# A four-layer graph network: memory and queue order at the start of the attention scores

## The reference, cut to what matters

```python
h = jnp.maximum(_layernorm(x), 0.0)
for head in range(8):
    Wx = h @ Ws[head] + Wb[head]
    s = Wx[v_tgt] @ a_w[head, :64] + Wx[v_src] @ a_w[head, 64:] + a_b[head]
    s = leaky_relu(s, 0.2)
    alpha = segment_softmax(s, v_tgt)
    outs.append(segment_sum(alpha[:, None] * Wx[v_src], v_tgt))
x = x + concat(outs)
```

## Time and profile before

| | us |
|---|---|
| median of 3 runs without the profiler | 2629.58 (2628.07 to 2631.13) |
| span of the profiled execution | 3086.3 |
| scoring and softmax in the profiled execution | about 2121 to 2482 |
| busy in it: PE, DVE, ACT, POOL | 2384.8, 1593.7, 335.0, 1795.9 |
| mean granted TensorE clock | 0.896 |

### The profile page before, as it was taken

One profiled execution on the slowest core, in us unless ns is written; L12 is line 12 of the kernel. 1 busy time (PEld: TensorE's weight loads), 2 busy tenths in 40 slices (PEclk: granted clock), 3 DMA queues, 4 the chain that ended last, 5 costly groups with the idle time before them and its releaser, 6 DMA issues.

```text
span 3086.3 us, 32808 instructions
## 1 busy us (share of the span) xinstructions
PE 2384.8 (77%) x8542; PEld 1265.4 (41%) x8542; DVE 1593.7 (52%) x3774; ACT 335.0 (11%) x523; POOL 1795.9 (58%) x1878
## 2 busy tenths in 40 slices
PE   7888889887678777785788888885068589988887
PEld 5534444343223222221354454453058445544444
DVE  7665555554234353332244444444059677766665
ACT  4200000000000000000000000001057310000000
POOL 0466666665466666665666666653710456666665
PEclk9898999998789888997899999997579789999999
DMA  6586666676567766666666666663134457776665
GB/s 157 174 243 180 174 180 177 187 241 177 154 192 212 203 201 205 196 193 181 184 200 198 204 200 199 204 181 80 10 101 153 136 157 211 208 222 192 194 190 171
DMA packets 212761, 557.12 MB, mean 181 GB/s; under 512 B 55433, under 2 KB 56834, under 8 KB 212601
## 3 DMA queue, kind: packets, MB, share of 16 engines
q0 software_dynamic: 144448, 462.60, 52.3%
q1 hardware_dynamic: 66970, 90.10, 9.7%
q10 hardware_dynamic: 1182, 2.33, 0.3%
HBM read 515.28 MB, written 39.59 MB: 180 GB/s over the span
## 4 chain that ended last, share of the span: by engine, by line
PE 51%; DVE 15%; another core or an unknown queue 13%; issue 12%; DMA 6%; POOL 2%; ACT 1%; SPq 0%; ACTq 0%; DVEq 0%; POOLq 0%
PE tiles L1456 28%; DMA ring<-table,src_t 5%; PE upper L1416 5%; PE last_bank L1597 2%; PE tiles L1453 2%; PE tiles L1452 2%; DVE sel L776 2%; PE upper L1458 2%; PE last_bank L1416 2%; PE upper L1687 1%; POOL ring L1758 1%; PE upper L1626 1%; PE upper L1405 1%; DVE stage L713 1%
## 5 line engine op out<-in xcount | busy, mean ns | idle before, releaser
L1758 POOL DMA_INDIRECT ring<-table,src_t x1320 | 1266.9, 960 | 717.8 <-issue 324.3
L1456 PE MATMUL tiles<-ring,sel 128*125 128x512 f32 x2590 | 1390.4, 652 | 264.2 <-issue 178.4
L1456 PEld LDWEIGHTS tiles<-ring,sel 128*125 128x125 f32 x2590 | 444.3, 198 | 754.6 <-issue 745.5
L1813 POOL DMA_INDIRECT ring<-table,src_t x415 | 399.0, 961 | 240.5 <-PE upper L1458 105.5
L483 DVE TENSOR_TENSOR sel<-iota_bank,dl_t 128x500 f32<-128x500 f32 (+1 forms) x330 | 221.5, 674 | 513.3 <-PE tiles L1456 226.6
L1218 DVE TENSOR_TENSOR ring<-ring,last_bank 128x512 f32<-128x512 f32 x388 | 260.5, 685 | 169.6 <-DMA ring<-table,src_t 140.6
L1458 PEld LDWEIGHTS upper<-big,sel 128*125 128x125 f32 x880 | 169.7, 193 | 222.5 <-issue 222.0
L1452 PE MATMUL tiles<-ring,sel 128*125 128x512 f16 x440 | 176.5, 401 | 61.8 <-issue 32.1
L1453 PE MATMUL tiles<-ring,sel 128*125 128x512 f16 x440 | 172.9, 393 | 10.6 <-issue 10.3
L1416 PE MATMUL upper<-wh,hTh 128*125 128x512 f32 x200 | 100.4, 502 | 73.1 <-DVE hTl L759 23.7
L1791 POOL DMA_INDIRECT big<-score_table,src_t x104 | 98.4, 946 | 81.5 <-DVE acc L988 50.1
(11 more groups left out here) (335 smaller groups left out, 2522.2 us busy)
## 6 DMA issues: line engine op xcount, KB each, us to landing
ring<-table,src_t POOLq DMA_INDIRECT x1735
table<-stage SPq DMA_DIRECT2D x50, 224.0 KB
table<-acc SPq DMA_DIRECT2D x50, 224.0 KB
acc<-dst_places SPq DMA_DIRECT2D x28, 256.0 KB
x<-dst_places SPq DMA_DIRECT2D x27, 256.0 KB
x<-in_x SPq DMA_DIRECT2D x25, 224.0 KB
kept_x<-x SPq DMA_DIRECT2D x25, 224.0 KB
x<-kept_x SPq DMA_DIRECT2D x25, 224.0 KB
```

The lines of the kernel that those rows point to most:

```text
L1456: last = P.matmul(to, sel[:, n % SELS, :], rows, start=False, stop=True, skip_group_check=True)
L1758: G.indirect_dma_start(out=(ring16 if layer == 2 else ring)[:, n % RING, :], out_offset=None, in_=table[layer][:, :], in_offset=bass.Indir ...
L1813: G.indirect_dma_start(out=rows_at(i), out_offset=None, in_=table[3][:, :], in_offset=bass.IndirectOffsetOnAxis(ap=src_t[:, i:i + 1], axis ...
```

## The change

- A tensor `spare` (12288 bytes in each partition) is added, and all six one-hot buffers lie in it. Its room comes from the descriptors' scratch, which is now 4096 bytes.
- DVE: the wait for the store of tile 22 ahead of `src_hot(0)` goes, and that for tile 23 ahead of the loop. The four masks move from ahead of `u3` to behind `rows_out` of tile 24.
- ACT: the waits for the stores of tiles 20 and 21 go; those for 22 to 24 move to the first `edge_scores`. The waits for `cont_ok` and `g1_z` move behind `dst_hot(2)`.
- POOL: the wait for `pj_out` moves from ahead of all gathers to ahead of the 65th. (The gathers of groups 3 to 31 write memory that holds no weights of the last projection; those from W3_GROUP = 35 do.)
- SP: the wait for `x_kept` and loads 2 and 3 move ahead of the stores of tiles 21 to 24; load 4 stays behind them.

```diff
+    W3_GROUP = next(k for k in GATHERED if (k + 1) * UG * H > KB * D)
...
+        spare = sb("spare", [128, 6, D])
...
-        dp, sp, dp_hot, sp_hot = ([flat_acc[:, 2 * WR + (2 * n + q) * GW // 2:2 * WR + (2 * n + q + 1) * GW // 2].bitcast(BF16)
-                                   for q in range(2)] for n in range(4))
+        dp, sp = ([flat_acc[:, 2 * WR + (2 * n + q) * GW // 2:2 * WR + (2 * n + q + 1) * GW // 2].bitcast(BF16)
+                   for q in range(2)] for n in range(2))
...
-        dp_hot.append(flat_acc[:, 3 * WR:3 * WR + GW // 2].bitcast(BF16))
-        sp_hot.append(stage[:, 9 * TH:9 * TH + GW // 2].bitcast(BF16))
+        dp_hot, sp_hot = ([spare[:, 3 * n + q, :].bitcast(BF16) for q in range(3)] for n in range(2))
...
-            stored(V, 22)
+            for k in range(TILES - LATE, TILES - 2):
+                rows_out(k)
             src_hot(0)
-            for to, flag, end in ((cont, keep, 0), (cont_back, nlast, CE - 1)):
...
             V.wait_ge(u_in, 48)
...
             rows_out(TILES - 2)
             rows_out(TILES - 1)
-            stored(V, TILES - 2)
+            for to, flag, end in ((cont, keep, 0), (cont_back, nlast, CE - 1)):
...
-            stored(A, 20)
             dst_hot(0)
-            stored(A, 21)
             dst_hot(1)
-            A.wait_ge(cont_ok, 2)
-            A.wait_ge(g1_z, TILES)
-            for t in range(TILES - 3, TILES):
-                stored(A, t)
 
             def edge_scores(b, half):
                 h0 = half * 4
+                if b == half == 0:
+                    for t in range(TILES - 3, TILES):
+                        stored(A, t)
...
                     dst_hot(k + 2)
+                if k == 0:
+                    A.wait_ge(cont_ok, 2)
+                    A.wait_ge(g1_z, TILES)
...
-            G.wait_ge(pj_out, 3 * TILES)
             for k in GATHERED:
+                if k == W3_GROUP:
+                    G.wait_ge(pj_out, 3 * TILES)
...
+            S.wait_ge(x_kept, 32 * TILES)
+            for k in range(2, NB):
+                load_dst(k)
+                load_src(k)
             for t in range(TILES - LATE, TILES):
                 store_rows3(t)
-
-            S.wait_ge(x_kept, 32 * TILES)
-            for k in range(2, 5):
-                load_dst(k)
-                load_src(k)
+            load_dst(NB)
+            load_src(NB)
...
-    nc = bacc.Bacc("TRN2", target_bir_lowering=False, num_devices=1)
+    nc = bacc.Bacc("TRN2", target_bir_lowering=False, num_devices=1, dynamic_dma_scratch_size=4096)
```

More of the change, by code:

```diff
@@ L1044, in vector_program @@
                                      scalar1=digit[:, 0:1], scalar2=-BIG, op0=ALU.not_equal, op1=ALU.mult))
-            for k in range(TILES - LATE, TILES - 2):
-                rows_out(k)
             def src_hot(k):
@@ L1072, in vector_program @@
             rows_out(TILES - 1)
-            stored(V, TILES - 2)
+            for to, flag, end in ((cont, keep, 0), (cont_back, nlast, CE - 1)):
+                own.mark(V.tensor_scalar(out=to, in0=flag, scalar1=-1.0, scalar2=2.0 * BIG, op0=ALU.add, op1=ALU.mult))
+                V.wait_ge(v_own, own.n)
+                V.memset(to[:, :, end:end + 1], -2.0 * BIG).then_inc(cont_ok, 1)
+            own.mark(V.tensor_scalar(out=pf, in0=pf, scalar1=-1.0, scalar2=BIG, op0=ALU.add, op1=ALU.mult))
+            V.tensor_scalar(out=pb_, in0=pb_, scalar1=-1.0, scalar2=BIG, op0=ALU.add, op1=ALU.mult).then_inc(flags_set, 1)
             def target_sum(c):
```

## The result

| | before | after |
|---|---|---|
| median without the profiler, 11 runs each, us | 2629.58 | 2618.02 |
| ratio after / before, 95% interval | | 0.9963 [0.9953, 0.9974] |
| profiled execution: span, us | 3086.3 | 2616.7 |

A forecast was written before the change was run, and what follows sets the result against it. The prediction took the scoring loop to be bound by DVE and PE in turn. Both starting 7.8 us earlier, with all else counted as nothing, gave 2629.6 - 7.8 = 2621.8 us, range 2614 to 2630.

The forecast's parts named there:

- The lower clock goes with the idle: PE's start of scoring: without its idle the lower clock goes, worth up to 1.5 us to PE, counted as nothing.
- The broadcasts in front: SP's loads 2 and 3 ahead of the late stores: load 2 there by 2120, load 3 by 2122.
- the wait for `x_kept`: SP, ahead of load 2: waiting for the last copy of x takes no more than 1 us.
- the slots leave at most 11 gathers unfinished: POOL's quarter scratch: by slot waits at most 11 gathers of a layer are unfinished, so nothing was taken.
- rival C: POOL, all four layers: the small scratch makes gathers wait for room, giving 2633 or 2790 us; chance 0.10.
- it is bound by DVE and PE in turn, and whatever lets both begin earlier moves its end: Steady scoring loop: DVE busy 113.18, PE 114.40 of 125 us; starting both 7.8 us earlier moves the end.
- The wait is covered by 2 us: ACT's dst_hot(3) behind cont_ok: ends by 2125, while PE needs it from 2127 on.
- cover of 2 to 3 us: Load 4, behind the stores: issued 6 us before, in time for src_hot(4) in group 3 at about 2130.
- ACT idle for `dst_places`: Start of scoring: ACT waiting for the places of a load, listed as a sign that the forecast was wrong.
- the signs of being right: Start of scoring: PE's 7.07 us idle gone, first score gather about 12 us ahead of the last rows_out, among others.
- The slow stretch: Scoring beside POOL's gathers in the first trace: 404 us of unexplained waits, taken to belong to the profiled execution only.
- rival A: Scoring: the gathers hold it in timed runs too, gain 11.9 to 14 us, 2616 to 2618; chance 0.13.

The follow-up runs named there:

- before_again: Kernel before, unchanged, timed against itself and profiled a second time: 2625.72 against 2625.35 us, ratio 1.0005, span 2619.7.
- loads_alone: Kernel before with only loads 2 and 3 and the wait for x_kept ahead of the stores of tiles 21 to 24: ratio 1.0003.
- the nine kernels of the table: The kernel before (profiled again), the kernel after and seven variants of these two, with ratios to before from 0.9961 to 1.0005.
- pool_wait_back: Kernel after with POOL's wait for pj_out back ahead of all score gathers: ratio 0.9961.
- gathers_alone: Kernel before with only POOL's wait for pj_out moved to the 65th score gather: ratio 0.9999.
- scratch_alone: Kernel before with only the descriptors' scratch cut to 4096 bytes: ratio 1.0001.
- masks_between: Kernel after with src_hot(1) and the four masks moved between the last two rows_out: ratio 0.9977.
- copies_later: Kernel after with ACT's eight mask copies moved behind later one-hots: ratio 0.9958, on a chip where before took 3089.32 us.
- all_three: Kernel after with masks_between, copies_later, and load 4 and load 5's places ahead of the late stores: 0.9951, where before took 3089.32 us.
- act_memory: loads_alone plus own memory for ACT's three one-hots and ACT's store waits moved as in after: 1.0008, where before took 3089.32 us.

## Why the prediction was right, and where it wasn't

**Size and sign.** 7.8 us forecast, 9.7 measured, 9.4 in the traces. Counted from the end of PE's last projection, as the forecast counts, the first maximum came 11.2 us behind by the earlier trace rows, 12.5 in `before_again` (DVE waited 3.75 us ahead of `src_hot(0)`, PE idled 2.62 ahead of the scoring where the earlier trace rows has 0.92) and 3.2 in after. That is 9.2 us for a gain of 9.4, and would look like proof of the forecast's account; loads_alone says that it isn't.

**The start, term by term.** PE begins the scoring right behind its projections (no idle, forecast 0), the masks and the two one-hots put the first maximum 3.2 us behind the projections' end (forecast 3.35), group 1 follows 4.0 us behind the projections' end (forecast 4.05), with 1.43 us of idle ahead of it (forecast none), since group 0 took 2.7 us and not 3.9. "The lower clock goes with the idle" held in groups 0 and 1: in the nine kernels of the table the group's first six matmuls of 224 columns took 1.28 us behind an idle of 5.31 to 7.70 us, at a granted clock of 0.50 and mostly 187 ns from one to the next (1.2 columns a ns), and 0.73 to 0.74 us behind 0 to 2.62 us of idle, at 1.00 and 95 ns from one to the next (2.4 columns a ns). The broadcasts in front serve `src_hot(2)` without a wait; the wait for `x_kept` cost nothing that shows.

**Gathers and scratch.** Priced at nothing, and in time nothing they were: pool_wait_back and gathers_alone, scratch_alone. The reason given for the scratch, that the slots leave at most 11 gathers unfinished, holds in the layers; the score gathers have no slots to wait for. In their train POOL does stop, as rival C has it, twice, 28 gathers apart, and for 2.1 to 4.7 us each; their price is hidden in the train's slack (`scratch_alone` 1.0001). No row of before shows how many gathers the small scratch holds; that it costs nothing was the author's estimate from the slots alone, and these stops are what the runs showed.

**The step that failed: "it is bound by DVE and PE in turn, and whatever lets both begin earlier moves its end".** I read that off a window of the late loop. In the first eight groups the engine with the longest chain is ACT (26.65 of 27 us), and it is ACT's start that the end followed: over the nine kernels of the table the time from the first maximum to the end is anything from 174.8 to 181.0 us, while from ACT's one-hot 5 to the end it is 167.7 to 169.9. (From one-hot 15 it is 142.9 to 145.1, but so late the 33rd maximum does as well, 149.2 to 151.6; that column alone would not single out ACT. PE's wait for one-hot 10 in all nine does.) loads_alone is the direct test: DVE's first maximum 3.1 us and PE's group 1 2.4 us earlier, ACT not, the end not. The earlier trace rows had ACT's wait of 11.24 us, and the sum has no term for it. So the forecast came out near by luck of the sizes: the change moves ACT's one-hot 15 by 7.7 us and the first maximum by 7.0. What made the gain is the part that I counted as by-work, ACT's waits for the stores, and it needs the order of the loads with it: order alone 1.0003, memory alone (with everything but the order) 0.9985, both 0.9963. ACT's one-hot 2 waits for a load and for the stores. Memory alone leaves the load; order alone brings the load early and pushes the stores back by 3 us, to the moment at which the load came before.

**A cover that wasn't.** "The wait is covered by 2 us", said of ACT's `dst_hot(3)` behind `cont_ok`, counted PE's need of one one-hot, not that ACT's chain was the bound: it stood 4.56 us for the masks, then 1.20 us for load 4, whose cover of 2 to 3 us I had counted for DVE alone. masks_between buys back the 4.56 us and gains 0.8 at the end, because it waits 1.14 for PE and its wait for load 4 grows to 3.29. "ACT idle for `dst_places`" was one of the forecast's own signs of being wrong, and it showed; of the signs of being right, the first gather came 9.8 us ahead of the last `rows_out`, not 12.

**The slow stretch.** I took it to belong to profiling, since its 404 us nearly make up the 456.7 that the timed runs lack; that was an estimate from two lengths, and no run showed it. The forecast for the timed runs was safe, as the 456.7 us weren't in them; the attribution is wrong. The profiled executions of nine kernels, `before_again` among them, show none of it (spans 2615.2 to 2631.7), and four kernels and the kernel before have it in their timed runs at 3077 to 3091 us. So profiling is neither needed for it nor enough. In that condition the runs fit rival A: 11 to 15 us measured for three variants of after, where it had 11.9 to 14; after itself wasn't run there.

**The rest of the 9.4 us.** 7.7 us are there by one-hot 15; the other 1.7 go with PE's granted clock. Behind one-hot 10 it fell in `before_again` (0.53 over 3 us, 26 matmuls) and not in after (1.00, 44). The same place in both (columns as in the earlier trace rows):

```profile
1912.00:1915.00 3.00, 3.00 (x26) 2.50 (x24) 2.21 (x5) 2.94 (x4) 2.39 (x3) 0.53 0.79 217
```

```profile
1910.80:1913.80 3.00, 3.00 (x44) 3.00 (x42) 3.00 (x7) 2.93 (x4) 2.39 (x3) 1.00 0.92 204
```

Of the nine kernels four have such a spell of some 3.4 us between one-hots 10 and 15, `pool_wait_back` among them, and 144.4 to 144.6 us from one-hot 15 to the end. Four have none and 142.9 to 143.2. `gathers_alone` has none there and 145.1, with a longer spell later. PE had idled 1.98 and 1.97 us ahead of step 80 in the two traces above, so that idle doesn't tell why; whether the timed runs hold these 1.7 us is open.

**Open.** That ACT's chain bounds the first groups rests on loads_alone, on the windows and on PE's waits in the traces; the runs that would have moved ACT alone fell in the other condition. Whether copies_later or all_three would beat after at 2626 wasn't measured: in their group all_three is the lowest, and its interval overlaps that of copies_later. No kernel here is shown to be better than after.

## What to carry to other kernels

To find what bounds the start of a pipelined loop, take the windows of its first groups and not of its steady part, and compare each engine's time for a group with all that it does only there, as ACT's copies of 0.60 us on top of 2.22. A buffer freed early and a transfer issued early can each be worth little or nothing and worth the gain together, when one instruction waits for both: follow every wait of that instruction before pricing either, and ask what a transfer put in front of the queue pushes back. A train with slack is worth nothing until something else stands still, so say in which condition the price holds.

## What the runs showed of the hardware

The condition of the earlier trace rows is not bound to the program or to profiling: the same kernel took 2626 us on two chips and 3089 on a third, and the first profile of before had it although the timed runs beside it (2629.58) had not. What sets it I can't say. In it PE's instructions come one by one while POOL issues indirect DMAs. Three of `act_memory`, inside the train, with "issue" as all that ends the idle:

```profile
2175.99 0.34 PE L1688 MATMUL upper<-stage 123*128 123x224 bf16 x1 [3.16 <-issue]
...
2179.48 0.35 PE L1688 MATMUL upper<-stage 123*128 123x224 bf16 x1 [3.15 <-issue]
...
2183.68 0.18 PE L1672 MATMUL tiles<-stage,spare 125*128 x1 [1.75 <-issue]
```

52 matmuls in 125 us are one in 2.4 us, at the lower clock (0.50), where 1314 matmuls in 140 us ran beside the same gathers elsewhere. Most gathers take 0.94 to 0.95 + 0.30 us in both conditions. What holds PE there no row shows.

A quarter of the scratch does make itself felt: two stops of POOL in the train of score gathers, of 2.1 to 4.7 us and 28 gathers apart, in all ten traces with 4096 bytes and in none of the four with 16384.

And the projections ahead of the scoring end 10.3 to 13.0 us from zero from one profile to the next with the same code, more than most terms of the sum.
